# One group at a time, all squares on ScalarE, odd tiles on VectorE: the last normalisation of a two-layer graph network

## The reference

```python
# layer 0
q, k, v = x @ Wq.T + bq, x @ Wk.T + bk, x @ Wv.T + bv
x = _layernorm(x + softmax(q @ k.T / sqrt(512) + adj + adj) @ v)
# layer 1: 8 heads of 64
feats = einsum('nf,hfd->hnd', x, W)
dense = leaky(e_self[:, :, None] + e_neigh[:, None, :]) + (-1e10 * (1 - adj))
x = _layernorm(x + relu(softmax(dense) @ feats + b))

def _layernorm(x, eps=1e-5):
    m = mean(x, -1); v = var(x, -1)
    return (x - m) / sqrt(v + eps)
```

## Time and profile before

| | |
|---|---|
| median of 3 runs | 1742.8 us (1739.8 to 1743.35) |
| the profiled execution | 1740.5 us, of which the span from the first to the last instruction is 1738.7 us |
| TensorE (PE) busy | 1631.4 us, 94% of the span |
| VectorE (DVE) busy | 1097.7 us, 63% |
| GpSimd (POOL) busy | 905.5 us, 52% |
| ScalarE (ACT) busy | 631.6 us, 36% |
| DMA | 298.27 MB, mean 172 GB/s |

### The profile page before, as it was taken

One profiled execution on the slowest core, in us unless ns is written; L12 is line 12 of the kernel. 1 busy time (PEld: TensorE's weight loads), 2 busy tenths in 40 slices (PEclk: granted clock), 3 DMA queues, 4 the chain that ended last, 5 costly groups with the idle time before them and its releaser, 6 DMA issues.

```text
span 1738.7 us, 22350 instructions
## 1 busy us (share of the span) xinstructions
PE 1631.4 (94%) x7748; PEld 749.6 (43%) x7748; DVE 1097.7 (63%) x1993; ACT 631.6 (36%) x1010; POOL 905.5 (52%) x859
## 2 busy tenths in 40 slices
PE   8989998999999999999999999999999999999920
PEld 3334443444444444444444444444444444444410
DVE  5454222766686768667866676667666776657455
ACT  4434321433343333333333333333333343335326
POOL 3000032666565656566656665665666566656352
PEclk9999999999999999999999999999999999999965
DMA  6443476576667676677667666866676667667247
GB/s 218 146 157 121 151 122 127 139 187 163 176 171 202 166 189 156 187 184 184 161 182 185 167 170 169 213 164 176 169 212 154 179 173 180 145 182 244 78 147 264
DMA packets 150483, 298.27 MB, mean 172 GB/s; under 512 B 16352, under 2 KB 16352, under 8 KB 147424
## 3 DMA queue, kind: packets, MB, share of 16 engines
q1 hardware_dynamic: 110944, 221.30, 38.1%
q0 software_dynamic: 39424, 75.52, 26.2%
HBM read 253.76 MB, written 42.99 MB: 171 GB/s over the span
## 4 chain that ended last, share of the span: by engine, by line
PE 85%; issue 4%; DVE 3%; POOL 3%; ACT 2%; DMA 1%; SPq 0%; POOLq 0%; DVEq 0%; ACTq 0%
PE S L524 37%; PE O L584 35%; PE O L524 5%; PE X L524 4%; POOL sacc L490 2%; PE O L595 1%; POOL ring L467 1%; DVE ring L1168 1%; ACT ring L850 1%; ACT xT L732 1%; PE X L636 1%; DMA ring<-in_xT 1%; DMA ring<-in_adjT 1%; PE BC L619 0%; DVE yb L1182 0%
## 5 line engine op out<-in xcount | busy, mean ns | idle before, releaser
L524 PE MATMUL S<-yb,xT 128*128 128x512 f16 x3072 | 699.8, 379 | 0.0
L584 PE MATMUL O<-vring,ring 128*128 128x512 f16 x2928 | 672.5, 380 | 4.2 <-DVE ring L996 3.0
L467 POOL DMA_DIRECT2D ring<-in_adjT x256 | 227.1, 887 | 448.6 <-ACT ring L732 420.2
L524 PEld LDWEIGHTS S<-yb,xT 128*128 128x128 f16 x3072 | 300.8, 98 | 366.0 <-issue 5.5
L584 PEld LDWEIGHTS O<-vring,ring 128*128 128x128 f16 x2928 | 285.6, 98 | 342.0 <-issue 6.2
L482 POOL TENSOR_TENSOR ring<-pf,ring 128x512 f16<-128x512 f32 x224 | 272.9, 1218 | 236.7 <-ACT ring L732 230.0
L732 ACT ACTIVATE ring<-S 128x512 f32<-128x512 f32 x256 | 152.5, 596 | 609.8 <-PE S L524 609.7
L490 POOL TENSOR_TENSOR sacc<-sacc,pf 128x512 f32<-128x512 f32 x248 | 343.8, 1386 | 29.3 <-ACT ring L732 26.0
L968 DVE MAX8 cand<-piece 128x8 f32<-128x512 f32 x256 | 176.2, 688 | 250.9 <-DMA piece<-in_adj 250.3
L1009 DVE TENSOR_TENSOR mx<-mx,ring 128x512 f32<-128x512 f32 x248 | 230.8, 931 | 79.1 <-DMA ring<-in_adjT 79.1
L787 ACT ACTIVATE pf<-ring 128x512 f32<-128x512 f32 x256 | 160.6, 627 | 269.4 <-DVE ring L992 261.4
(11 more groups left out here) (116 smaller groups left out, 793.6 us busy)
## 6 DMA issues: line engine op xcount, KB each, us to landing
ring<-in_adjT POOLq DMA_DIRECT2D x256, 256.0 KB, 4.3
piece<-in_adj SPq DMA_DIRECT2D x256, 256.0 KB, 4.3
vring<-v_scratch SPq DMA_DIRECT2D x244, 256.0 KB, 3.7
ring<-in_xT SPq DMA_DIRECT2D x8, 1024.0 KB, 7.4
v_scratch<-vring SPq DMA_DIRECT2D x32, 256.0 KB, 2.0
y_scratch<-yb SPq DMA_DIRECT2D x8, 1024.0 KB, 4.9
yb<-y_scratch SPq DMA_DIRECT2D x8, 1024.0 KB, 7.4
xr<-in_x SPq DMA_DIRECT2D x32, 256.0 KB, 5.3
```

Of the source, the lines that this page charges most:

```text
L467: pool.dma_start(ring[:, c % SLOTS, :], adj_t[k * P:(k + 1) * P, b * QB:(b + 1) * QB], accum_op=ALU.add).then_inc(adj_in[c % 4], 16)
L524: mm = pe.matmul(psum, sta(a, k), mov(b, k), start=(k + a + b == 0), stop=(k == n - 1 and a == 1))
L584: mm = pe.matmul(O[j][:, :], ring16[:, e % SLOTS, a, j * P:(j + 1) * P], vring[:, e % NV, m, :], start=(k + a + m == 0), stop=(k == NT - 1 ...
```

## The change

`BY_SQUARES` and `TOGETHER` go. All nine groups are treated alike and alone: VectorE adds and makes the negative mean, ScalarE squares all of the group's tiles and takes the square root, VectorE makes the scale and the shift. The BatchNorm statistics and their aggregation disappear. ScalarE normalises only the first, third, ... tile of each group, VectorE the second, fourth, ... one, directly behind the shift of that group. VectorE does so for group e-1 after the additions of group e, and ScalarE normalises its tiles of group e-1 after the squares and the square root of group e. SyncE waits for both counters, `e_out` and `e_out_odd`, before it stores a group.

```diff
             for tiles in GROUPS:
                 first, last = tiles[0], tiles[-1] + 1
-                sp.wait_ge(e_out, min(last, NT - 1))
-                if last == NT:
-                    sp.wait_ge(e_out_last, 1)
+                sp.wait_ge(e_out, last // 2)
+                sp.wait_ge(e_out_odd, last // 2)
                 sp.dma_start(out[first * P:last * P, :] ...
...
+            def normalise(e):
+                act.wait_ge(e_rstd, e + 1)
+                for t in GROUPS[e][::2]:
+                    nc.scalar.activation(got[:, t, :], got[:, t, :], ACT.Identity, bias=e_nm[:, t:t + 1],
+                                         scale=e_r[:, t:t + 1]).then_inc(e_out, 1)
+
+            for e, tiles in enumerate(GROUPS):
+                first, last = tiles[0], tiles[-1] + 1
+                act.wait_ge(e_neg, e + 1)
+                for t in tiles:
+                    nc.scalar.activation(O[t % JB][:, :], got[:, t, :], ACT.Square, bias=e_mean[:, t, 0:1],
+                                         scale=1.0 / float(D) ** 0.5, accum_out=e_mean[:, t, 1:2]).then_inc(e_square, 1)
+                act.wait_ge(e_square, last)
                 nc.scalar.activation(e_s[:, first:last], e_mean[:, first:last, 1], ACT.Sqrt, bias=eps[:, :],
                                      scale=1.0).then_inc(e_sd, 1)
+                if e >= 1:
+                    normalise(e - 1)
+            normalise(NE - 1)
...
-            def last_rstd(k):
+            def last_rstd(e):
...
+                dve.scalar_tensor_tensor(out=e_nm[:, t], in0=e_mean[:, t, 0], scalar=float(D) ** 0.5, in1=e_r[:, t],
+                                         op0=ALU.mult, op1=ALU.mult).then_inc(e_rstd, 1)
+                dve.wait_ge(e_rstd, e + 1)
+                for t in range(first + 1, last, 2):
+                    dve.tensor_scalar(got[:, t, :], got[:, t, :], e_r[:, t:t + 1], e_nm[:, t:t + 1], ALU.mult, ALU.add
+                                      ).then_inc(e_out_odd, 1)
...
-                    if e in BY_SQUARES:
-                        dve.wait_ge(e_sum, last)
-                        dve.tensor_scalar(e_mean[:, first:last, 0], e_tot[:, first:last], -1.0 / float(D) ** 1.5, None,
-                                          ALU.mult).then_inc(e_neg, 1)
-                        continue
-                    for k in range(len(TOGETHER)):
-                        if TOGETHER[k][-1] == e - 1:
-                            last_rstd(k)
...
-                    for t in tiles:
-                        dve.wait_ge(e_sum, t + 1)
-                        dve.bn_stats(e_st[:, t, :], got[:, t, :]).then_inc(stats_set, 1)
-                    for n, t in enumerate(tiles):
-                        dve.wait_ge(stats_set, NT + counted + n + 1)
-                        dve.bn_aggr(e_mean[:, t, :], e_st[:, t, :]).then_inc(mv_set, 1)
-                last_rstd(len(TOGETHER) - 1)
-                dve.tensor_scalar(got[:, NT - 1, :], got[:, NT - 1, :], e_mean[:, NT - 1, 0:1], e_r[:, NT - 1:NT],
-                                  ALU.subtract, ALU.mult).then_inc(e_out_last, 1)
+                    dve.wait_ge(e_sum, last)
+                    dve.tensor_scalar(e_mean[:, first:last, 0], e_tot[:, first:last], -1.0 / float(D) ** 1.5, None,
+                                      ALU.mult).then_inc(e_neg, 1)
+                    if e >= 1:
+                        last_rstd(e - 1)
+                last_rstd(NE - 1)
```

More of the change, by code:

```diff
@@ L205, in adj_resnorm_kernel @@
         GROUPS = [range(e * JB, (e + 1) * JB) for e in range(NB - 1)] + [range(NT - JB, NT - 2), range(NT - 2, NT)]
-        BY_SQUARES = (1, 3, 5)
-        TOGETHER = ((0, 1), (2, 3), (4, 5), (6,), (7,), (8,))
         x1r_in = [sem(f"x1r_in{e}") for e in range(NB - 1)]
         got_in = [sem(f"got_in{e}") for e in range(NE)]
-        e_neg, e_square, e_sum, e_sd, e_chain, e_rstd, e_out, e_out_last, out_done = map(
-            sem, ("e_neg", "e_square", "e_sum", "e_sd", "e_chain", "e_rstd", "e_out", "e_out_last",
+        e_neg, e_square, e_sum, e_sd, e_chain, e_rstd, e_out, e_out_odd, out_done = map(
+            sem, ("e_neg", "e_square", "e_sum", "e_sd", "e_chain", "e_rstd", "e_out", "e_out_odd",
                   "out_done"))
@@ L216, in adj_resnorm_kernel @@
         end = yb[:, 1].bitcast(F32).rearrange("p a c n -> p (a c n)")
-        e_st = end[:, 0:NT * 6].rearrange("p (t s) -> p t s", s=6)
         e_mean = end[:, 256:256 + 2 * NT].rearrange("p (t s) -> p t s", s=2)
@@ L864, in _ @@
-            normalise(len(TOGETHER) - 1)
+                if e >= 1:
+                    normalise(e - 1)
+            normalise(NE - 1)
             def general():
@@ L1138, in prove_single @@
                 then(dve.tensor_reduce(okw[:, 0:1], gap, AX.X, ALU.add))
-            def last_rstd(k):
-                t = slice(GROUPS[TOGETHER[k][0]][0], GROUPS[TOGETHER[k][-1]][-1] + 1)
-                dve.wait_ge(e_sd, k + 1)
+            def last_rstd(e):
+                first, last = GROUPS[e][0], GROUPS[e][-1] + 1
+                t = slice(first, last)
+                dve.wait_ge(e_sd, e + 1)
                 dve.reciprocal(e_r[:, t], e_s[:, t]).then_inc(e_chain, 1)
-                dve.wait_ge(e_chain, k * 4 + 1)
+                dve.wait_ge(e_chain, e * 4 + 1)
                 dve.scalar_tensor_tensor(out=e_t[:, t], in0=e_mean[:, t, 1], scalar=EPS, in1=e_r[:, t], op0=ALU.add,
                                          op1=ALU.mult).then_inc(e_chain, 1)
-                dve.wait_ge(e_chain, k * 4 + 2)
+                dve.wait_ge(e_chain, e * 4 + 2)
                 dve.scalar_tensor_tensor(out=e_t[:, t], in0=e_t[:, t], scalar=-0.5, in1=e_r[:, t], op0=ALU.mult,
                                          op1=ALU.mult).then_inc(e_chain, 1)
-                dve.wait_ge(e_chain, k * 4 + 3)
+                dve.wait_ge(e_chain, e * 4 + 3)
                 dve.scalar_tensor_tensor(out=e_r[:, t], in0=e_t[:, t], scalar=1.5, in1=e_r[:, t], op0=ALU.add,
                                          op1=ALU.mult).then_inc(e_chain, 1)
[L1153 to L1159, removed]
+                dve.wait_ge(e_chain, e * 4 + 4)
+                dve.scalar_tensor_tensor(out=e_nm[:, t], in0=e_mean[:, t, 0], scalar=float(D) ** 0.5, in1=e_r[:, t],
[4 more added lines that the diff above has]
+                                      ).then_inc(e_out_odd, 1)
             def last_norm():
@@ L1170, in last_norm @@
                                                  accum_out=e_tot[:, t:t + 1]).then_inc(e_sum, 1)
-                    if e in BY_SQUARES:
-                        dve.wait_ge(e_sum, last)
-                        dve.tensor_scalar(e_mean[:, first:last, 0], e_tot[:, first:last], -1.0 / float(D) ** 1.5, None,
-                                          ALU.mult).then_inc(e_neg, 1)
-                        continue
-                    for k in range(len(TOGETHER)):
-                        if TOGETHER[k][-1] == e - 1:
-                            last_rstd(k)
-                    counted = sum(len(GROUPS[i]) for i in range(e) if i not in BY_SQUARES)
-                    for t in tiles:
-                        dve.wait_ge(e_sum, t + 1)
-                        dve.bn_stats(e_st[:, t, :], got[:, t, :]).then_inc(stats_set, 1)
-                    for n, t in enumerate(tiles):
-                        dve.wait_ge(stats_set, NT + counted + n + 1)
-                        dve.bn_aggr(e_mean[:, t, :], e_st[:, t, :]).then_inc(mv_set, 1)
-                last_rstd(len(TOGETHER) - 1)
-                dve.tensor_scalar(got[:, NT - 1, :], got[:, NT - 1, :], e_mean[:, NT - 1, 0:1], e_r[:, NT - 1:NT],
-                                  ALU.subtract, ALU.mult).then_inc(e_out_last, 1)
+                    dve.wait_ge(e_sum, last)
[4 more added lines that the diff above has]
+                last_rstd(NE - 1)
             prove_single()
```

## The result

The changed kernel takes 1735.05 us, the median of 7 runs (1727.21 to 1738.95), against 1742.62 us of 7 runs before: ratio 0.9958, 95% interval 0.9939 to 0.9976. It is faster, by 7.6 us in the medians. Two later comparisons of the same two kernels gave 0.9973 (0.9959 to 0.9986) and 0.9975 (0.9962 to 0.9989), so some 4 to 5 us: the sign is clear of the noise in all three, the size is between 0.25 and 0.4% by their middle values.

A forecast was written before the change was run, and what follows sets the result against it. ScalarE's backlog, which holds up the stores, was taken to bound the end. Last tile 1722.3 plus tail 7.3 plus stall 1 gave a span of 1730.6 us, 8.1 less time: 1742.8 to 1734.7 us, range 1729 to 1743.

The forecast's parts named there:

- the 8.1 us: Whole kernel: forecast gain, from a profiled execution of 1740.5 us to one of 1732.4 us.
- The rhythm and the tail: Last stage: VectorE 4.8 and ScalarE 4.7 us a group, gathers every 5.2; last tile at 1722.3, end 7.3 us later.
- First store: SyncE's store of group 0: to leave at about 1687.2 us instead of 1699.39.
- The DMA rate of 342 GB/s: Gathers and stores together from 1687.2 us: 12.85 MB at this rate take 37.6 us, ending no earlier than 1724.8.
- The port: VectorE's normalised tiles beside GpSimd's gathers: bounds 0.54 and 1.45 us a tile, 0.54 taken.
- rival C: Last stage: twelve VectorE tiles cost 0.91 us more each, 1735.2 us, or GpSimd is held up, 1738.5; chance 0.10.
- the hole in the DMA's work: Before the change, after 1711.5 us: DMA 6% busy for 6 us, as stores wait for work in ScalarE's queue.
- the backlog: ScalarE before the change: never idle from 1711.3 to 1731.4 us, because two groups share one square root.
- I take 1 us net: VectorE's unexplained stall while gathers and stores meet: a few us absorbed, 1 us added, making the span 1730.6 us.
- rival D: Stalls as dense as before, over 8 us of VectorE idle without releaser: 1741.6 us, no change; chance 0.17.
- E: VectorE at a third of its rate where gathers and stores meet, over 15 us idle: 1747.6 us, slower; chance 0.11.

The follow-up runs named there:

- once_more: The changed kernel unaltered, run again on chip C where VectorE shows no stall: 1728.91 us, ratio 0.9975 to the kernel before.
- hold_stores: The changed kernel with SyncE waiting for all 32 gathers before its first store: 1735.60 us, ratio 0.9981 to the kernel before.
- plain_pool: The changed kernel with GpSimd's 32 gathers by index replaced with plain loads of the same size on the same queue, indexing left out: 1718.87 us.
- pad64: The changed kernel with 64 empty instructions in VectorE's stream ahead of the last stage: 1734.01 us, ratio 0.9976 to the kernel before.
- one_sum: The changed kernel with only the last addition of each group raising the semaphore: 1733.63 us, ratio 0.9964 to the kernel before.
- wait_all: The changed kernel with VectorE waiting for all 32 gathers before its first addition of the last stage: one run, 1759.81 us.

## Why the prediction was right, and where it wasn't

**The time and the sign.** 1734.7 us was forecast and 1735.05 measured. The ratio asked for was 0.9953; the first comparison has it in its interval, the two repetitions (0.9973 and 0.9975) don't. The gain is rather half to nine tenths of the 8.1 us. That the time came out within 0.4 us is luck in good part: the forecast puts 1730.6 - 1666.5 = 64.1 us between the first gather and the end, and the two profiles with a stall took 71.3 and 72.0. In the profiled executions the span became only 1.5 us shorter (1738.7 to 1737.2); it was the medians of the first comparison that lay 7.6 us apart.

**The rhythm and the tail: right.** I put the last tile 1722.3 - 1666.5 = 55.8 us behind the first gather. Without the stall (once_more) it is 1719.22 - 1664.16 = 55.1. First store forecast 20.7 us after the first gather, measured 20.2 in both profiles. The rest from last tile to end was put at 7.3 us, measured 6.7. The DMA rate of 342 GB/s was measured as 349 and 337. One reading under it was weak: the landing times of the earlier trace rows, 3.8 us and at most 6.5, are those of 6 of the 32 gathers, the only ones whose landing that trace holds in full. In once_more, which holds all 32, they are 3.3/4.6/10.1 us (min/median/max); the last one landed 1710.1 - 1704.4 = 5.7 us after its issue, near the 6.3 that I took. The port: 0.545 us a tile, so the low bound of the earlier trace rows held and rival C is out. By the rule of the Trainium skill, "SBUF — State Buffer", section on who interferes with whom, the tiles, if they run in a two-port mode, should have kept GpSimd from writing descriptors; its issues took 942 ns at the least and 944 in the middle, against 945 and 949 before, so a lock-out isn't to be seen in them. The trace doesn't tell whether the tiles ran in such a mode.

**Where the gain comes from.** Taking each group alone brings 3.2 us on chip C, where the whole change brings 4.0, and these two can't be told apart. With the squares on ScalarE but without VectorE's share of the tiles nothing is gained (0.9997). The whole kernel loses nothing that can be told apart when its stores are held back (hold_stores, 0.9981 beside 0.9973). That the hole in the DMA's work was a sign of the backlog in ScalarE, and not the loss itself, fits this but isn't shown, since that kernel's stall was shorter too.

**The stall: mis-sized, and of another cause.** The step "I take 1 us net" failed. The stall is 12.0 us in the first profile and 13.7 in the repetition, over the 8 us that I had set as the sign of rival D, and under E's 15; in the first profile the last tile is 64.5 us behind the first gather, just as in the kernel before with 64.9. I had subtracted a tail almost without stall from a profiled execution that holds one. D was closer on the stall's size, but its time, 1741.6 us and no change, was wrong: it let the change alone bear the extra stall. The times say that both kernels bear about as much. From chip A to chip C the kernel before goes from 1739.67 to 1732.88 us and the changed one from 1735.62 to 1728.91, 6.8 and 6.7 us. For the changed kernel the profiles show that this lies in the last stage (72.0 and 61.7 us from the first gather to the end). Of the kernel before there is no profile on chip C, so that its 6.8 us are the stall too is inferred. Why its 6.0 us of stall would cost as much as 12 isn't shown either; ScalarE's backlog behind it, 20 us without a gap, leaves it no room to recover.

**The cause of the stall** isn't settled. Shown: it needs no stores and comes with DMA engines 71% busy (hold_stores); full DMA engines don't bring it by themselves (plain_pool, once_more); it isn't bound to a place in VectorE's stream (pad64), and its long gap doesn't need four semaphore updates for a group (one_sum). It is absent when VectorE works after the gathers by index (wait_all) or beside plain loads. It begins 26 to 33 us after the first gather and is over some 5 us after the last one's issue. It was in all seven profiles in which VectorE worked beside 32 gathers by index outside chip C (for the first two profiles the chip isn't known), and in none of the three on chip C.

The traces hold one more trail, the recorded times of the semaphore updates. In the changed kernel's first profile the updates of group 4's four additions, which end from 1697.5 to 1699.3 us, are recorded at 1699.2, 1701.3, 1703.4 and 1706.2, and the mean starts with the last. So the updates themselves come late, one after the other. And many are recorded not at all: of the 64 updates with which the gathers of group 4 report their landing the trace has 4, where once_more's has 64. In all seven profiles with a stall 293 to 385 of 15840 updates by DMAs are missing, all of them in the last stage, and 27 to 39 of some 3900 updates by engines. In wait_all, on chip B, 207 updates by DMAs are missing too, though VectorE, which only waits there, shows no stall. None is missing on chip C, nor with the plain loads on chip B. So what goes wrong hits the semaphore updates of DMAs and engines alike while gathers by index run, and on chip B it is there even without work on VectorE. That the recording of these events takes part in it is a rival that no run excludes. Open is what on a chip decides it, and whether it is the index or the 40 us of GpSimd's issuing; an equally slow row of plain loads, which would tell these apart, wasn't run.

## What to carry to other kernels

Work that is joined to save small instructions, here two groups to one square root, delays what stands behind it in a strict queue; look for an engine that is first idle and then full to the end, and take the units apart. Moving work to that engine paid here only with as much taken off it elsewhere. And when a forecast is made against a profile with an unexplained idle time, put at least the same idle time on both sides of the subtraction.

## What the runs showed that I had not expected

- VectorE can stand for 6 to 8 us between an addition that is recorded as finished and the instruction that waits for it, with GpSimd issuing indexed gathers about every 1.3 us and no other engine or DMA that the profile names. The updates that it waits for are recorded 2 us and more apart.
- Whether it does differed between the chips of these runs. The times of both kernels differed with it by 6.7 and 6.8 us of 1740, more than the change brings; how much of that is the stall is shown for the changed kernel's last stage alone. Ratios within one chip agreed (0.9973 and 0.9975) where times between chips differed by 0.4%.
- Plain loads of the same 8.39 MB take 17.1 us of GpSimd's issuing where gathers by index take 40, and the whole kernel is then 1718.9 us, with 54.3 us from the first load to the end. The changed kernel with its gathers takes 61.7 without a stall and 69.3 to 72.0 with one. So the gathers' pace is worth some 7 us of this stage, and the stall 8 to 10 more.
